# Attention features of a one-core block: exponential and clamp over two PSUM banks at a time

## What is computed

```python
def attn(x):                                  # linear attention, 16 heads of 8, 128 features a head
    q, k, v = split(x @ W_qkv.T, 3)
    q_p = elu(einsum('bhnd,hdf->bhnf', q, proj)) + 1.0
    k_p = elu(einsum('bhnd,hdf->bhnf', k, proj)) + 1.0
    kv = einsum('bhnf,bhnd->bhfd', k_p, v)
    z = 1.0 / (einsum('bhnf,bhf->bhn', q_p, k_p.sum(axis=2)) + 1e-08)
    return (einsum('bhnf,bhfd->bhnd', q_p, kv) * z) @ W_out.T + b_out

def ffn(x):                                   # 8 experts (128 -> 512 -> 128), the best 2 weighted
    weights = top2_mask(softmax(x @ w_router))
    h = gelu(einsum('te,ieh->tih', x, w1) + b1)
    return sum_i((einsum('tih,ihe->tie', h, w2) + b2) * weights)

x = x + attn(layernorm(x))
x = x + ffn(layernorm(x))
```

## Time and profile before

| | |
|---|---|
| median of 3 runs | 368.87 us (367.48 to 372.21) |
| span of the profiled execution, first to last instruction | 365.0 us |
| the profiled execution's own time | not listed; the median is 3.9 us above the span |
| busy: TensorE / VectorE / ScalarE / GpSimd | 320.5 / 275.2 / 227.7 / 104.8 us |
| start to first feature matmul | 55.3 us |
| attention stage, eight passes | 55.3 to 159.1 us |
| experts, to the end | 159.1 to 365.0 us |

### The profile page before, as it was taken

How to read it: one execution, slowest core, us unless ns; L and a number is a source line. 1 busy time by engine, 2 the same in 40 slices (tenths; PEclk the granted TensorE clock), 3 DMA queues, 4 the chain that set the end, 5 groups by cost and what they waited for, 6 DMA issues and landing times.

```text
span 365.0 us, 6770 instructions
## 1 busy us (share of the span) xinstructions
PE 320.5 (88%) x1994; PEld 222.6 (61%) x1994; DVE 275.2 (75%) x547; ACT 227.7 (62%) x409; POOL 104.8 (29%) x114
## 2 busy tenths in 40 slices
PE   6300478999999999999989999999999999999996
PEld 2000445455555556476858777877777777877775
DVE  4000796989899998976696988788887888778884
ACT  1000546888988898867765666666666666666660
POOL 3000462126236425530447412022120212202120
PEclk9555598999999999988999999999999999999999
DMA  3204043133435234000220111020111201022121
GB/s 99 79 26 144 18 96 79 44 103 89 110 108 129 66 107 115 0 2 2 64 54 29 57 35 59 29 90 32 54 50 38 86 32 57 29 57 70 45 55 31
DMA packets 19047, 22.53 MB, mean 62 GB/s; under 512 B 2993, under 2 KB 13777, under 8 KB 18929
## 3 DMA queue, kind: packets, MB, share of 16 engines
q1 hardware_dynamic: 19026, 22.28, 21.7%
HBM read 14.85 MB, written 1.11 MB: 44 GB/s over the span
## 4 chain that ended last, share of the span: by engine, by line
PE 80%; DMA 10%; DVE 4%; ACT 3%; issue 2%; SPq 1%; ACTq 0%
PE feat_ps L972 24%; PE mix_ps L990 13%; PE x_ps L990 12%; DMA x_all<-x 10%; PE feat_ps L855 6%; PE kv_ps L868 5%; PE at_ps L875 5%; PE feat_ps L859 4%; PE mix_ps L899 2%; DVE proj_st L492 1%; ACT exps L731 1%; PE mix_ps L885 1%; PE kv_ps L958 1%; PE mix_ps L832 1%; PE kv_ps L997 1%
## 5 line engine op out<-in xcount | busy, mean ns | idle before, releaser
L778 ACT ACTIVATE feats<-feat_ps,b_s 128x512 f32<-128x512 f32 x128 | 88.3, 690 | 65.9 <-PE feat_ps L972 65.1
L538 DVE SCALAR_TENSOR_TENSOR feats<-exps,feat_ps 128x512 f32<-128x512 f32 x128 | 84.5, 679 | 10.5 <-ACT exps L731 7.4
L731 ACT ACTIVATE exps<-feat_ps 128x512 f32<-128x512 f32 x128 | 74.7, 611 | 16.6 <-PE feat_ps L859 8.5
L445 POOL TENSOR_TENSOR feats<-feats 128x512 f32<-128x512 f32 x26 | 33.9, 1302 | 128.1 <-DVE feats L667 128.1
L648 DVE CAST qk_hi<-feats 128x512 fp32r<-128x512 f32 x64 | 44.4, 694 | 28.7 <-ACT feats L778 28.6
L972 PE MATMUL feat_ps<-qk_hi,w_hi 128*128 128x512 f32 (+1 forms) x128 | 52.3, 409 | 0.0
L972 PE MATMUL feat_ps<-qk_lo,w_hi 128*128 128x512 f32 (+1 forms) x128 | 51.0, 398 | 0.0
L972 PE MATMUL feat_ps<-qk_hi,w_lo 128*128 128x512 f32 (+1 forms) x128 | 50.8, 397 | 0.0
L650 DVE TENSOR_TENSOR qk_lo<-feats,qk_hi 128x512 fp32r<-128x512 f32 x64 | 44.9, 702 | 2.8
L653 DVE TENSOR_TENSOR qk_lo<-feats,qk_hi 128x512 fp32r<-128x512 f32 x64 | 43.9, 686 | 0.0
L792 ACT CAST qk_hi<-feats 128x512 fp32r<-128x512 f32 x64 | 39.1, 611 | 0.0
(11 more groups left out here) (111 smaller groups left out, 497.8 us busy)
## 6 DMA issues: line engine op xcount, KB each, us to landing
exps<-gates_dram SPq DMA_DIRECT2D x32, 256.0 KB, 3.1
w_raw<-wcat SPq DMA_DIRECT2D x8, 512.0 KB, 3.6
stack<-qk_hi SPq DMA_DIRECT2D x64, 64.0 KB, 2.0
stack<-qk_lo SPq DMA_DIRECT2D x32, 64.0 KB, 2.0
out<-res SPq DMA_DIRECT2D x4, 256.0 KB, 3.5
feats<-proj SPq DMA_DIRECT2D x1, 776.0 KB
x_all<-x SPq DMA_DIRECT2D x2, 256.0 KB, 3.2
x_all<-x SPq DMA_DIRECT2D x1, 512.0 KB, 35.8
```

Source lines behind the costliest of these rows:

```text
L538: dve.scalar_tensor_tensor(out=feats[:, u % FR, :], in0=exps[:, u % RING, :], scalar=1.0, in1=feat_ps[:, u % RING, :], op0=ALU.min, op1=AL ...
L731: act.activation(exps[:, u % RING, :], feat_ps[:, u % RING, :], ACT.Exp, bias=-1.0).then_inc(exp_done, 1)
L778: act.activation(gel[:, c, :], feat_ps[:, c, :], ACT.Gelu_apprx_tanh, bias=b1_s[:, e, c:c + 1]).then_inc(gelu_done, 1)
```

## The change

At odd units only, ScalarE takes the exponential of two banks (128x1024) and VectorE clamps the same two banks; even units have neither. `exp_done` and `feat_done` count pairs. The banks are the same four, as pairs (0,1) and (2,3). TensorE waits at even units only, for the pair before the last one, so before unit u it waits for units u - 4 and u - 3. The other work keeps its place in every engine's order; at an even unit it no longer has a clamp or exponential of that unit ahead of it.

```diff
+UP = U // 2
@@ VectorE, body(b, ...), for u in range(U):
-                    dve.wait_ge(exp_done, b * U + (u + 1))
-                    if not (isinstance(b, int) and b * U + u < FR):
-                        dve.wait_ge(feat_used, b * U + (u + 1 - FR))
-                    dve.scalar_tensor_tensor(out=feats[:, u % FR, :], in0=exps[:, u % RING, :], scalar=1.0,
-                                             in1=feat_ps[:, u % RING, :], op0=ALU.min, op1=ALU.max
-                                             ).then_inc(feat_done, 1)
+                    if u % 2:
+                        dve.wait_ge(exp_done, b * UP + (u // 2 + 1))
+                        if not (isinstance(b, int) and b * U + u < FR):
+                            dve.wait_ge(feat_used, b * U + (u + 1 - FR))
+                        two, pair = (u - 1) % RING, (u - 1) % FR
+                        dve.scalar_tensor_tensor(out=feats[:, pair:pair + 2, :], in0=exps[:, two:two + 2, :],
+                                                 scalar=1.0, in1=feat_ps[:, two:two + 2, :], op0=ALU.min,
+                                                 op1=ALU.max).then_inc(feat_done, 1)
@@ ScalarE, body(b, ...)
-                    if units:
+                    if units and u % 2:
+                        two = (u - 1) % RING
                         act.wait_ge(feat_mm, b * U + (u + 1))
-                        act.activation(exps[:, u % RING, :], feat_ps[:, u % RING, :], ACT.Exp,
+                        act.activation(exps[:, two:two + 2, :], feat_ps[:, two:two + 2, :], ACT.Exp,
                                        bias=-1.0).then_inc(exp_done, 1)
@@ TensorE, body(b, ...)
-                        if not (isinstance(b, int) and b * U + u < RING):
-                            pe.wait_ge(feat_done, b * U + (u + 1 - RING))
+                        if u % 2 == 0 and not (isinstance(b, int) and b * U + u < RING):
+                            pe.wait_ge(feat_done, b * UP + (u // 2 - 1))
                         feature(k, u)
@@ TensorE, after the passes
-            pe.wait_ge(feat_done, B * U)
+            pe.wait_ge(feat_done, B * UP)
```

## The result

The changed kernel took 402.6 us (median of 4 runs, 398.5 to 403.5), the kernel before 370.5 us in the same comparison. The ratio is 1.094 (1.085 to 1.102); it leaves out runs in a slower state, such as one of 378.0 us of the kernel before. It is slower, by about twice as much as forecast (385 us, range 377 to 391). The profiled execution took 403.5 us with a span of 401.5, 36.5 us over the span before.

The account below looks back on a forecast made before the run. The prediction took TensorE's own order to bound the attention stage. Waits of 1.97 us in seven passes plus 2.6 in the first add 16.4 us to 368.9, giving 385 us, range 377 to 391.

Parts of the forecast that it names:

- the third rival: New TensorE gaps of 1.2 us twice a pass lower its clock: 15 us more, time about 400; chance 0.06.
- the clock at 1.00 through the stage: Expected sign in the profile after: TensorE's granted clock stays at 1.00 (2.4 GHz) through the attention stage.
- The ring: Pairs 1, 3, 5 and 7 share banks, so four bank returns plus TensorE's stretches between allow no pass under 14.82 us.
- The wait before unit 2: TensorE has 1.10 us of other work there against 2.37 needed, so it waits 1.27 us in seven passes.
- The cover at unit 2: In the kernel before, each clamp was said to end about 0.5 us or more before the matmul waiting for it.
- The way: From an odd unit's last matmul through wide exponential and clamp to the next matmul into that pair: 2.37 us.
- A pass: Each attention-stage pass but the first grows from 12.97 by 1.97 us of waits to 14.94 us.
- Next to no reserve: Even units 4 to 12 would wait for next to nothing, but have no reserve either.
- The first two passes: The first pass ends some 2.6 us later, bounds 0.7 and 3.5; the second grows by 1.97 us.
- The engines' savings: Rival: wide clamps save VectorE 0.07 us a pair, 4.5 us over 64 pairs, time 364; chance 0.04.
- One of the two waits is hidden: Rival: only one wait of about 1.1 us a pass, before unit 2 or 14, remains; 377 to 378 us; chance 0.08.
- The ring with longer ways: Rival: wide instructions cost two narrow ones, a pair's return takes 2.72 us, time 396 (11 us more); chance 0.12.

Follow-up runs that it names:

- e4_gap: The kernel before, all narrow, with TensorE waiting two banks sooner than needed before units 2 and 14; 446.6 us.
- e1_fill: The changed kernel with 512-column matmuls that nobody reads added where TensorE waits, in every pass; 385.8 us.
- e5: The changed kernel with the exponential narrow again, clamp wide, waits in pairs, and matmuls that nobody reads in TensorE's gaps; 378.2 us.
- e6: The changed kernel with the clamp narrow again, exponential wide, a wait for each unit, and matmuls that nobody reads in the gaps; 379.7 us.
- e2: The changed kernel with the matmuls of units u and u + 1 directly after each other at even units; 376.8 us.
- e7: The changed kernel with a pair's matmuls side by side, plus matmuls that nobody reads ahead of and in the first pass; 371.3 us.
- e11_wide_start_fill: The changed kernel with matmuls that nobody reads only ahead of and in the first pass, later gaps left empty; 395.8 us.
- e8_before_warm: The kernel before with matmuls that nobody reads ahead of the first pass and behind every second logit matmul; 368.5 us.

## Why the prediction was wrong

**The step that failed** is the one of the third rival, "TensorE's clock falls (0.06)", and the line in the list of signs, "the clock at 1.00 through the stage". The prediction held that gaps of 1.2 us don't lower the clock, since it had fallen after 2.9 us of standstill and had stayed up in a window busy 1.70 of 2.00. It falls with them: at 132 and 184 us of the changed kernel behind gaps of 1.2 us, and at 64 behind one of 1.7. So the sum put the clock at nothing, and it cost 16.6 of the 36.2 us. The price of the rival was about right (15 us, time 400; measured 16.6 and 402.6), but by luck: it took a quarter of every pass at the low clock, and what came was the second pass and most of the first and the fifth, at 6 to 7 us for a whole pass, with the others at or near 1.00. Its chance was too low, and the range ended at 391 because of the chance. Two rows said what the clock does; that neither stands close to the gaps of the new kernel should have left the rival at a third or more, with the range up to 400.

The reading itself had a hole. I took idle time as what counts. In the trace before, the clock was already at 0.50 while the attention rounds ran behind the logits, and TensorE had not been idle from 158 us to its fall at 161: the twelve logit matmuls of 8 columns (24 in the trace) began at 159. So the clock can fall in a stretch that is counted busy. And the other way round, a low clock makes every matmul longer and the busy share full (2.00 of 2.00 at 66 us), so that a full share is no sign that TensorE has more to do. The Trainium skill's rule on small gaps ("TensorE: Matmul & The Clock Gate", A second HAM failure mode), which the prediction cited and put aside, says that the clock goes up and down with them. The changed kernel's trace agrees, with three falls and three returns in the passes after 61 us; e4_gap's doesn't, where it stayed down (23.73 against 15.07 us a pass with the gaps filled).

**The ring, point by point.** With the gaps filled, e1_fill took 385.8 us against 385 forecast. That is closer than the terms deserve, and partly luck: its waits are 3.2 us over the forecast, and the forecast took the kernel before at 368.9 us where e1_fill's comparison has 367.4, and left the experts as they were, which took 1.6 us less.

- The wide instructions: 1.01 and 1.22 taken, 1.03 and 1.22 measured.
- The wait before unit 2: 1.27 forecast, 1.23 measured as idle time.
- The cover at unit 2: taken as free of waits, with each clamp half a microsecond early. That isn't so there: in the earlier trace rows the first of the two clamps ends at 120.66, and unit 2's weights load at 120.71, after 0.31 us of waiting for it.
- The way: 2.37 forecast, 2.46 measured from unit 11 to unit 14 and from unit 15 to unit 2. The hand-over from exponential to clamp was 0.11 us (exponential from 170.70 to 171.73, clamp at 171.84) and not 0.03.
- A pass: 14.94 forecast, 15.40 measured. "Next to no reserve" at units 4, 8 and 12 was right, and with the longer way it became waits of 0.1 to 0.2 us there. "TensorE's busy time unchanged near 12.7" was not: 13.5.
- The first two passes: 4.6 forecast (2.6 and 1.97), 5.0 measured in e1_fill (3.0 and 1.98).
- Together: 16.4 forecast, 19.6 measured.
- e5 and e6 give the slope from there: a way shorter by 0.4 or 0.6 us takes 1.2 us off a pass.

**The other rivals.** The engines' savings (364 us) had no part: VectorE and ScalarE were 3 to 4 us less busy each and waited longer. "One of the two waits is hidden" didn't happen. The ring with longer ways was right by a third of its price (3.2 of 11 us).

## What to carry to other kernels

A wide instruction on a ring of banks saves its engine a little (1.22 against twice 0.68 us here) and makes each bank's way longer by what it takes over a narrow one (0.42 and 0.54 us here); what decides is whether the producer has as much other work between filling a pair and wanting the one before. Work that out place by place in the order, from the rows, as was done here, and then ask what the gaps do to TensorE's clock: two gaps of about a microsecond in a pass cost 2.1 to 2.4 us as waits and, in a pass at the low clock, 6 to 9 us more. Cheap matmuls into an idle bank help to tell which of the two a time is, if the granted clock is read beside them: in e6 they didn't hold it. Putting the matmuls of two units side by side took 0.9 us off TensorE's busy time, and with narrow instructions it left 0.4 us of idle time in a pass.

## What was not expected of the hardware

- Matmuls that nobody reads make a kernel faster: e1_fill against the changed kernel, 385.8 against 402.6 us.
- The clock can stay at 0.50 through a whole stage in which TensorE is shown busy 22.1 of 23.7 us a pass (e4_gap), and for 32 us in which it is shown busy without a break (e6_clamp_narrow_fill).
- As much idle time did not lower it in shorter pieces: 1.7 us a pass in stretches of at most 0.62 us left it at 1.00 in all later passes of e2 and e7.
- Alike passes with alike gaps go either way: four at 1.00, the last at 0.56 (e11_wide_start_fill).
- A 512-column matmul behind every second logit matmul of 8 columns didn't hold the clock: it fell at 162 us, before the last of them, and was at 0.53 in the mean from 162 to 164 (e8_before_warm).
- The order alone is worth 0.9 us of TensorE's busy time a pass: 12.7 alternating, 11.8 side by side, with the same matmuls.
